# Transformer layer on one core: GpSimd's product of the attention output one chunk further ahead, VectorE's third product between statistics and their gathering, transposes one down tile later

## The reference

```python
x = _layernorm(x + attention(x, W_qkv, W_proj))      # causal, 16 heads of 16, d = 256
x = _layernorm(x + ffn(x, w_gate, w_up, w_down))     # h = silu(gate) * up, 768 wide
# ffn, weights are integers times 1/127:
gate = jnp.einsum('bsd,hd->bsh', x, wg)
up = jnp.einsum('bsd,hd->bsh', x, wu)
h = jax.nn.silu(gate) * up
return jnp.einsum('bsh,dh->bsd', h, wd)
```

## Time and profile before

| | us |
|---|---|
| runs of the kernel, median of 3 | 1343.06 |
| lowest, highest | 1338.88, 1343.30 |
| the profiled execution's own time | 1337.92 |
| its span, first to last instruction | 1335.4 |

### The profile page before, as it was taken

One profiled execution on the slowest core, in us unless ns is written; L12 is line 12 of the kernel. 1 busy time (PEld: TensorE's weight loads), 2 busy tenths in 40 slices (PEclk: granted clock), 3 DMA queues, 4 the chain that ended last, 5 costly groups with the idle time before them and its releaser, 6 DMA issues.

```text
span 1335.4 us, 28651 instructions
## 1 busy us (share of the span) xinstructions
PE 1236.8 (93%) x11348; PEld 593.9 (44%) x11348; DVE 1078.9 (81%) x1526; ACT 873.6 (65%) x1734; POOL 383.4 (29%) x464
## 2 busy tenths in 40 slices
PE   4999988999999999999999989999989898989897
PEld 2665643333333333333333333333355656565554
DVE  5687768989889988999988988988357777777776
ACT  2655557888888888888878778788734343333333
POOL 3000002212222132132221222221235555554544
PEclk7999989999999999999999999999989999999999
DMA  5798521221312433223122123120031332323221
GB/s 196 238 294 246 179 88 50 68 80 51 96 52 63 110 104 96 68 57 93 50 67 83 50 62 87 50 67 27 17 107 64 96 94 90 101 84 107 80 63 48
DMA packets 130293, 124.36 MB, mean 93 GB/s; under 512 B 47456, under 2 KB 101216, under 8 KB 130160
## 3 DMA queue, kind: packets, MB, share of 16 engines
q1 hardware_dynamic: 130160, 122.54, 31.0%
HBM read 71.04 MB, written 50.86 MB: 91 GB/s over the span
## 4 chain that ended last, share of the span: by engine, by line
PE 67%; DVE 11%; ACT 7%; POOL 6%; issue 4%; DMA 3%; SPq 1%; POOLq 0%; DVEq 0%; ACTq 0%
PE ps L1321 18%; PE ps L1304 12%; PE ps L1386 11%; DVE row_max L971 6%; PE ps L1224 6%; PE ps L1207 5%; PE ps L1338 4%; ACT probs L840 4%; PE ps L1229 4%; POOL h_lo L735 3%; PE ps L1251 2%; POOL v_sb L712 2%; DMA q_stack<-max_rows 2%; PE ps L1297 2%; SPq L555 1%
## 5 line engine op out<-in xcount | busy, mean ns | idle before, releaser
L971 DVE TENSOR_REDUCE row_max<-ps 128x2 f32<-128x1024 f32 (+1 forms) x512 | 567.1, 1152 | 42.6 <-PE ps L1229 25.6
L840 ACT ACTIVATE probs<-ps 128x512 f32<-128x512 f32 (+1 forms) x1024 | 506.7, 589 | 96.6 <-PE ps L1304 96.3
L707 POOL TENSOR_SCALAR_AFFINE_SELECT probs<-probs 128x512 f32<-128x512 f32 x256 | 162.8, 637 | 624.2 <-ACT probs L840 534.5
L1321 PE MATMUL ps<-probs,v_ones 128*32 128x512 f32 (+3 forms) x3072 | 328.7, 500 | 10.2 <-issue 8.9
L1304 PE MATMUL ps<-q_stack,k_stack 50*128 50x512 f16 (+1 forms) x1024 | 309.6, 371 | 15.3 <-DMA q_stack<-max_rows 10.4
L1224 PE MATMUL ps<-k_stack,q_stack 48*128 48x512 f16 (+3 forms) x1536 | 306.1, 329 | 11.3 <-DVE row_max L971 10.7
L874 ACT ACTIVATE silu<-ps 128x512 f32<-128x512 f32 x96 | 57.4, 597 | 197.3 <-PE ps L1386 197.3
L1304 PEld LDWEIGHTS ps<-q_stack,k_stack 50*128 50x128 f16 x1024 | 88.5, 93 | 211.0 <-ACT probs L840 174.5
L1229 PE MATMUL ps<-above,one_of_half 64*128 64x64 bf16 (+1 forms) x2048 | 165.8, 203 | 0.0
L735 POOL TENSOR_TENSOR h_lo<-h_sb,h_hi 128x512 f16<-128x512 f32 x96 | 119.4, 1250 | 150.7 <-ACT h_hi L882 150.7
L968 DVE TENSOR_REDUCE row_max<-ps 128x4 f32<-128x1024 f32 (+1 forms) x128 | 122.3, 955 | 34.0 <-PE ps L1229 33.2
(11 more groups left out here) (125 smaller groups left out, 1449.4 us busy)
## 6 DMA issues: line engine op xcount, KB each, us to landing
x_sb<-in_L_attn_x SPq DMA_DIRECT2D x32, 512.0 KB, 5.2
qk_parts<-parts SPq DMA_DIRECT2D x64, 256.0 KB, 3.5
attn_t<-o_sb SPq DMA_DIRECT2D x64, 256.0 KB, 2.8
q_stack<-qk_parts SPq DMA_DIRECT2D x192, 64.0 KB, 2.3
k_stack<-qk_parts SPq DMA_DIRECT2D x192, 64.0 KB, 2.3
v_rows<-v_sb SPq DMA_DIRECT2D x16, 512.0 KB, 3.2
v_flat<-v_rows SPq DMA_DIRECT2D x32, 256.0 KB, 3.5
v_sb<-attn_t SPq DMA_DIRECT2D x32, 256.0 KB
```

Source lines behind the costliest of these rows:

```text
L707: pool.affine_select(out=tile, in_=tile, compare_op=ALU.is_ge, fill=0.0, base=0, pattern=[[0, HG], [1, P]], channel_multiplier=-1).then_in ...
L840: act.activation(tile[:, j, 0:w], ps[:, 4 + use % 3, 0:w], ACT.Exp, scale=scale_of_batch).then_inc(exp_done, 1)
L971: dve.tensor_reduce(row_max[:, half, :, p, qt], banks[:, :, 0:w], AX.X, ALU.max).then_inc(s_free, 1)
L1321: last = pe.matmul(ps[32 * j:32 * j + 32, 7, c0:c0 + w * P], v_ones[n % 2][:, kt, j, :], probs[(NS * n + s) % RING][:, j, 0:w * P], start= ...
```

## The change

Four things are moved, and nothing is added or taken away. On GpSimd, `scale_attn(c+3)` stands at the end of chunk c in place of `scale_attn(c+2)`, with the same wait for `out_ready` at c, and `scale_attn(2)` stands ahead of chunk 0. Also on GpSimd, `inverse_deviation` of the first norm stands ahead of the fourth low part in place of the third. On VectorE, `hidden(c, 2)` stands between `ln_stats` and `ln_variance`. On TensorE, the high transposes stand ahead of down tile 2 in place of 1, the low ones ahead of down tile 4 in place of 3. SyncE's and ScalarE's programs stay as they were.

```diff
-        TURN_HI, TURN_LO = 1, 3
+        TURN_HI, TURN_LO = 2, 4
...
             def chunk_c(c, has_prev, has_next):
                 for hc in range(HC):
-                    if hc == 2 and has_next:
+                    if hc == 3 and has_next:
                         inverse_deviation(0, ln1_step, c + 1)
...
-                if c + 2 < NCH:
+                if c + 3 < NCH:
                     if has_prev:
                         pool.wait_ge(out_ready, c)
-                    scale_attn(c + 2)
-
+                    scale_attn(c + 3)
+
+            scale_attn(2)
             chunk_c(0, False, True)
...
                     ln_stats(0, ln1_step, n, x1[npar], range(TILES))
+                hidden(c, 2)
+                if has_next:
                     ln_variance(0, ln1_step, n)
-                hidden(c, 2)
                 hidden(c, 3)
```

## The result

The changed kernel takes 1402.97 us (median of four runs, 1399.71 to 1405.28), the kernel before 1340.97 in the same comparison (1337.83 to 1343.30). The ratio is 1.0462, 95% interval 1.0426 to 1.0498: 62 us slower. The forecast was 1422 with a range of 1404 to 1446; the direction is right, the measured median lies 1 us under the range.

A forecast was written before the change was run, and what follows sets the result against it. A loop through three engines, from R over the first normalisation to the next R, was taken to bound each 22.46 us chunk. 76.8 + 2.3 + 1.7 + 0.2 = 81.0 on 1337.9 gives 1419, plus 3: 1422, range 1404 to 1446.

The forecast's parts named there:

- The completion: Loads of chunk c+3, queued behind the store on SyncE, were to be complete at R + 11.7, between 11.0 and 12.5.
- R: The moment VectorE ends `ln_apply(1)`, the normalisation of z, in a chunk; the store waits for it.
- the first normalisation of 3.09 us ends at 21.75: VectorE's normalisation of x in the new loop, 3.09 us as before, was to end 21.75 us after R.
- 2.3 + 1.7 = 4.0: Start of the stage: chunk 0 2.3 us later by the product of chunk 2 ahead, chunk 1 1.7 by later `rstd`.
- The last chunks: Chunk 14, without the projection's wait: `rstd` behind the third low part was to come 0.2 us late.
- the first pause: TensorE's wait for hidden product 3, until about R + 16, over 4 us; the clock was forecast to fall here, losing nothing.
- the second pause: TensorE's wait for ScalarE's cast, R + 19.6 to R + 23, over 3 us; sign: over 2 us.
- the transposes at nothing: TensorE's transposes one tile later were to change nothing, within 0.3 us a chunk to either side.
- Rival (a): TensorE's clock at half behind the second pause in each chunk: 24 us on top, 1446; chance 0.12.
- (b): Loads in time; later `rstd` gives back the 1.45 us a chunk of the projection's wait: near 1347; chance 0.05.
- (c): Loads in time and `rstd` not held by the third low part; waits of projection and gate tile 4 go: 1323; chance 0.03.
- Rival (d): GpSimd's wait lasts but the loads end sooner, at R + 9, 12 x 2.7 less: 1390; chance 0.06.

The follow-up runs named there:

- one small edit alone: The kernel before with only the transposes one down tile later (1341.89 us, 0.9993), or only hidden product 2 moved between statistics and gathering (1343.07 us, 1.0005).
- the rest of the findings: Loads ahead of the store, `rstd` behind two low parts, low parts 2 and 3 behind the normalisation of x, third product ahead of the gathering: 1315.21 us, 0.9797.

## Why the prediction came out as it did

**Right: which wait takes the place of the removed one.** The loads behind the store were the reason, and they alone: with the product ahead and nothing else the kernel takes 1404.2 us, with the loads taken out of the store's way 1333.85. The completion was taken at R + 11.7, and the product starts at R + 11.51 on average; the bounds of 11.0 and 12.5 hold 9 of 12 chunks. The tail from the end of the first normalisation to the next R was taken from the trace of before as 6.99 us and is 6.99 (1159.31 to 1166.30).

**Wrong: "the first normalisation of 3.09 us ends at 21.75".** The change itself moves `rstd` behind the third low part, so one low part and not two stands beside the normalisation, which then takes 2.21 us. The earlier trace rows had what was needed: `rstd` at 1142.55 to 1143.56, the normalisation from 1143.60, and the same instruction four times in 1.38 us on z with nothing on GpSimd beside it. What the 3.09 holds is two instructions of VectorE that last until a low part is done: 1143.92 to 1145.17 beside one that ends at 1145.02, and 1145.42 to 1146.68 beside one that ends at 1146.54. I carried a duration over into a place with other neighbours. The terms of the loop:

| per chunk, us | predicted | measured |
|---|---|---|
| store to product | 11.7 | 11.51 |
| product, three low parts, `rstd` | 6.95 | 6.64 |
| normalisation of x, with its start | 3.10 | 2.25 |
| from there to R, and handovers | 7.10 | 6.99 |
| sum | 28.85 | 27.39 |

The stores were to be 28 to 30 us apart and are 26.8 to 28.6. The difference of 1.45 us is 17.4 in twelve chunks, of which the normalisation is 10.2, more than all the rest. In the second line the low parts take 1.11 each from start to start and not 1.16, and the handover behind the product is no term of its own, since the next instruction starts 2.30 us after it.

Of the ends, the start was forecast at 2.3 + 1.7 = 4.0 and is 3.4. That this is near is in part luck. The product of chunk 2, for which I took 983.3, that is 12.3 us behind the stage's first transposes, comes at 14.5, with the last of its loads issued at the same place in both kernels (4.5 us behind those transposes before, 4.4 after):

```profile
992.67 2.36 POOL L712 TENSOR_TENSOR v_sb<-v_sb,recips 128x1024 f32<-128x1024 f32 x1 [16.65 <-DMA recips<-attn_recips]
```

So the dip of the DMA share in the earlier trace rows was not the end of these loads, and `rstd` of chunk 0 is 4.5 us late and not 2.3. At the `rstd` of chunk 1 the delay is 4.3, where 4.0 had been forecast; from there to the first store the shorter normalisation takes 0.9 off.

The last chunks were forecast at +0.2 and are at -1.5. In chunk 14 `rstd` is 0.3 late, as forecast, but the chunk is 0.6 shorter than before (21.88 against 22.47): again the 0.88 of the normalisation. The other 0.9 lie between the stores of chunks 13 and 14 (14.39 against 15.26) and had no price. They don't come of the product ahead (15.26 with it alone); the other three edits give them without it (14.38), and the transposes alone give 0.4 (14.89). Why is not shown.

By sum: 81.0 - 17.4 - 0.6 - 1.7 = 61.3, and 61.1 is what the profiled execution shows. The 3 us that I added for the median were there: the median of before is 3.05 above its profiled execution, and 1337.9 + 61.1 + 3 = 1402, against 1402.97. The lower end of the range had no ground in the terms either: they give 1422 - 8 - 4 = 1410, not 1404. With the normalisation at 2.21 and all else as written the forecast would have been 1412.

**Right: the clock takes its drop in the first pause.** That pause came, 3.3 to 5.2 us long. TensorE behind it, and the stretches of the chunk (columns as above):

```profile
1154.75 0.39 PE L1388 MATMUL ps<-x_hi,wgate_t 128*128 128x512 f16 x1 [4.28 <-DVE h_sb L1118]
```

```profile
1154.73:1158.40 3.67, 3.65 (x11) 1.58 (x12) 1.30 (x2) 1.21 (x2) 3.46 (x4) 0.56 0.01 2
1158.40:1166.30 7.90, 7.54 (x70) 5.96 (x68) 7.19 (x21) 3.39 (x5) 3.80 (x3) 0.99 0.01 2
```

The clock is at 1.2 GHz for nearly all of the first stretch and back at 2.4 in the second. In the 3.6 us from 4.3 us behind the product's start it is between 0.50 and 0.69 in each of the twelve chunks. The slow matmuls fill what would have been the second pause: the transposes wait 0.36 us in the shown chunk and 0.53 at most, where a sign named in the prediction was over 2 us. Rival (a), 24 us more, did not occur. The rule of the Trainium skill that the clock drops when the array idles ("TensorE: Matmul & The Clock Gate", Part 1) holds in every chunk here. It cost nothing in this kernel. In one chunk (product at 1179.01) the clock is at 0.50 from 1182.6 to 1189.2, longer than in the others, and from its product to the next store it is 15.90 us as everywhere.

**Right: the transposes at nothing.** The kernel before with them moved alone is at 0.9993.

**Rivals (b) and (c), the loads in time.** The kernel with the loads ahead of the store is this case made real. I had given it two prices: 1347, with the 1.45 us of the projection's wait given back by the later `rstd` and 0.2 more, or 1323. It is 1333.85: the product ahead gains 1.30 a chunk and the later `rstd` costs 0.70, not 1.65. The 0.88 us by which the normalisation is shorter are missing there too. One overlooked pair of neighbours made both the forecast and this rival too slow. Rival (d), the loads at R + 9, did not occur.

**What stays open.** The completion of the last gather scatters from 10.8 to 13.1 us after the store, from chunk to chunk and with the same issues; no run here tells why. The share of the edits in chunk 0 is known only from one execution of each kernel: from the first transposes to the first store 47.8 us before, 50.7 with the product ahead alone, 48.7 with the other three alone, 51.2 with all four, where kernels with one small edit alone have 46.7 and 47.1.

## What to carry to other kernels

When an operation is moved to use data one step earlier, look first on whose queue its load stands and behind which wait: a load issued behind a store inherits the store's wait. Then price every moved instruction with the neighbours it will have: on VectorE and GpSimd a duration belongs to a pair of instructions (look at the single ones, not at the sum of four), and a wait that keeps the two apart can be worth more than it costs. If the product ahead is wanted, move its loads ahead of the store first; with that the same change went from 4.6% slower to 0.7% faster, and with the rest of the findings to 2% faster.

## What the runs showed of the hardware

**VectorE beside GpSimd.** Four `tensor_scalar` of 128x256 f32 take 1.38 us alone, 2.21 with one subtraction of 128x512 on GpSimd beside them, 3.04 to 3.10 with two, and 3.40 beside the product of 128x1024. In the sums this looks like a slower VectorE. The single instructions say otherwise. Each takes 0.40 to 0.42 us, or it takes 1.2 us and more, and then it ends 0.15 us behind an instruction of GpSimd; over the kernels here that is so for all 253 long ones (0.146 to 0.154). In each of them the instruction of GpSimd had begun first. So it holds one instruction of VectorE until it is done.

It also goes the other way. The last two low parts of a chunk take 2.79 us, where two take 2.27 ahead of `rstd`. The first of the two begins while VectorE is at the low half of x:

```profile
1160.42 1.22 DVE L1107 TENSOR_TENSOR x_lo_rows<-x,x_hi_rows 128x1024 f16<-128x1024 f32 x1
1160.98 1.68 POOL L735 TENSOR_TENSOR h_lo<-h_sb,h_hi 128x512 f16<-128x512 f32 x1 [2.79 <-ACT h_hi L883]
```

It takes 1.68 us instead of 1.16; the one behind it takes 1.15. In the kernel before, low part 2 begins 0.2 us behind an instruction of the normalisation and takes 1.23.

**The clock behind short waits.** With TensorE waiting 1.29 us a chunk the clock stayed at 2.4 GHz throughout. At 2.15 us it was at half in 4 of 12 chunks, and at 1.98 us (for `z_sb`) in 6 of 12, with the fall costing 1.7 us each time; in the kernel after, with 3.3 us and more of waiting, in 12 of 12. The wait that grew from 1.29 to 2.15 us lengthened the chunk by 0.70 us where the clock held and by 2.38 where it fell.
